# Two-part branch, tile 2's gate/up inside tile 1's second layer, and a last tile in column halves, in a macaron block on one core

## What is computed

```python
def ffn(x):                       # weights ternary, hidden width 512, every linear layer without bias
    h = silu(lin(x, w1) * w1_s) * (lin(x, w2) * w2_s)
    h = gelu(lin(h, h1) * h1_s)   # 512 -> 512
    h = gelu(lin(h, h2) * h2_s)   # 512 -> 512
    return lin(h, w3) * w3_s      # 512 -> 128
x = x + 0.5 * ffn(layernorm(x))
h = layer_norm(layernorm(x), gamma, beta)
k, v = lin(h, Wk) + bk, lin(h, Wv) + bv
w = exp((lin(k, Wka) + bka) / sqrt(128)); w = w / cumsum(w)
x = x + cumsum(w * k) * v         # cumsums along the 256 positions
x = x + 0.5 * ffn(layernorm(x))
```

## Time and profile before

| | us |
|---|---|
| median of 3 runs | 395.91 (395.11 to 396.01) |
| the profiled execution | 396.45 |
| its span in the trace | 394.7 |
| PE busy | 382.2 (97%) |
| DVE busy | 337.2 (85%) |
| ACT busy | 304.7 (77%) |
| POOL busy | 49.9 (13%) |

### The profile page before, as it was taken

How to read it: one execution, slowest core, us unless ns; L and a number is a source line. 1 busy time by engine, 2 the same in 40 slices (tenths; PEclk the granted TensorE clock), 3 DMA queues, 4 the chain that set the end, 5 groups by cost and what they waited for, 6 DMA issues and landing times.

```text
span 394.7 us, 5879 instructions
## 1 busy us (share of the span) xinstructions
PE 382.2 (97%) x1670; PEld 292.7 (74%) x1670; DVE 337.2 (85%) x755; ACT 304.7 (77%) x513; POOL 49.9 (13%) x70
## 2 busy tenths in 40 slices
PE   7789999999999999999999999999999999999995
PEld 2367888777777787777687787777777777778883
DVE  4868778989989899998999899799899989976733
ACT  2767778996896799679779986877898778686763
POOL 4721011110100220101022010100411010020000
PEclk9999999999999999999999999999999999999999
DMA  7700000000000000000000000000000000000001
GB/s 265 261 1 2 0 2 0 1 0 2 0 2 0 0 0 0 0 0 0 0 0 0 0 0 27 0 0 27 0 0 27 0 27 0 27 2 0 27 2 55
DMA packets 3901, 7.45 MB, mean 19 GB/s; under 512 B 560, under 2 KB 1200, under 8 KB 3760
## 3 DMA queue, kind: packets, MB, share of 16 engines
q1 hardware_dynamic: 3168, 6.36, 4.5%
q10 hardware_dynamic: 720, 0.93, 0.7%
HBM read 5.19 MB, written 2.10 MB: 18 GB/s over the span
## 4 chain that ended last, share of the span: by engine, by line
PE 79%; DVE 11%; issue 4%; ACT 4%; POOL 0%; DVEq 0%; ACTq 0%; POOLq 0%
PE hid_ps L385 52%; PE gate_ps L385 6%; PE up_ps L385 5%; PE y_ps L385 5%; DVE rcsum L783 3%; PE y_ps L397 3%; PE xt_ps L397 2%; PE y_ps L521 2%; PE xt_ps L505 2%; DVE gate L700 1%; DVE csum L778 1%; ACT L632 1%; DVE full L710 1%; ACT full L572 1%; PE xt_ps L508 1%
## 5 line engine op out<-in xcount | busy, mean ns | idle before, releaser
L385 PE MATMUL hid_ps<-act_hi,hi_h 128*128 128x512 f32 x512 | 208.9, 408 | 1.0 <-DVE flag_i L661 1.0
L385 PE MATMUL hid_ps<-act_lo,hi_h 128*128 128x512 f32 x512 | 200.1, 391 | 0.0
L719 DVE TENSOR_TENSOR act_lo<-full,act_hi 128x512 fp32r<-128x512 f32 x189 | 124.2, 686 | 27.5 <-ACT act_hi L577 21.9
L572 ACT ACTIVATE full<-hid_ps,vec 128x512 f32<-128x512 f32 x128 | 88.0, 688 | 43.3 <-PE hid_ps L385 38.9
L385 PEld LDWEIGHTS hid_ps<-act_hi,hi_h 128*128 128x128 f32 x512 | 96.2, 188 | 25.3 <-issue 4.9
L385 PEld LDWEIGHTS hid_ps<-act_lo,hi_h 128*128 128x128 f32 x512 | 96.2, 188 | 23.0 <-issue 3.8
L577 ACT ACTIVATE act_hi<-full 128x512 fp32r<-128x512 f32 x128 | 79.4, 629 | 6.6 <-POOL nmr L287 5.3
L285 POOL TENSOR_TENSOR rstd<-veps,half 128x4 f32<-128x4 f32 x24 | 32.0, 1334 | 294.4 <-DVE veps L680 294.4
L710 DVE SCALAR_TENSOR_TENSOR full<-up_ps,s_half,gate 128x512 f32<-128x512 f32 x63 | 47.1, 748 | 1.5
L555 ACT ACTIVATE tanh<-gate_ps,s_half 128x512 f32<-128x512 f32 x63 | 42.4, 683 | 7.5 <-PE gate_ps L385 6.1
L560 ACT ACTIVATE act_hi<-full 128x512 fp32r<-128x512 f32 x64 | 40.2, 627 | 6.7 <-DVE full L710 6.4
(11 more groups left out here) (80 smaller groups left out, 347.9 us busy)
## 6 DMA issues: line engine op xcount, KB each, us to landing
out<-x_sb SPq DMA_DIRECT2D x8, 256.0 KB, 2.0
x_sb<-x SPq DMA_DIRECT2D x1, 1536.0 KB, 6.5
raw_h<-h2t SPq DMA_DIRECT2D x4, 256.0 KB, 6.9
raw_h<-h1t SPq DMA_DIRECT2D x2, 256.0 KB, 5.3
raw_h<-h1t ACTq DMA_DIRECT2D x2, 256.0 KB, 6.7
raw_w<-w2t ACTq DMA_DIRECT2D x1, 256.0 KB, 4.5
raw_w<-w1t SPq DMA_DIRECT2D x1, 256.0 KB, 4.3
x_sb<-x SPq DMA_DIRECT2D x1, 256.0 KB, 6.7
```

Of the source, the lines that this page charges most:

```text
L385: mm = eng.matmul(ps, w, a, start=(first and n == 0), stop=(last and n == len(seq_) - 1))
L572: eng.activation(full23[m % 2][:, :], hid_ps[m % 2][:, :], ACT.Gelu, scale=col("sh1" if n == 2 else "sh2", m)).then_inc(s_gelu[n], 1)
L719: eng.tensor_tensor(act_lo[n][:, m, :], full[m % 2][:, :], act_hi[n][:, m, :].bitcast(F32), ALU.subtract).then_inc(s_lo[n], 1)
```

## The change

It has five parts. **Warm-up**: seven products instead of ten, four at once, two behind the first `veps`, one behind POOL's first power. **Flags**: the weights' bits are looked at by other engines and at other times, with two flags, one for w1, w2, h1 and one for h2, w3; PE branches twice. **Order**: between the two branches stands SECOND_LAYER, in which pass 1's transposes and gate/up products p1.0 to p1.2 lie among pass 0's second layer, whose first two chunks are taken input by input (p2a to p2d, one of the four inputs each). Pass 1's statistics and normalisation move ahead into START on all engines, POOL's norm(1) moves ahead of low1.0, the h2 casts behind the low1's, and pass 1's tile is loaded before h1.2. Pass 1's first-layer result gets buffers of its own ("second"). **Last tile**: chunk 3 of pass 15's third layer, its w3 product, the transposes back, the add and the store are done in two halves of 256 columns; the fourth input of the w3 product is taken in plain float32 straight from the gelu's result (`last_p4_end`), without `high3.3` and `low3.3`; ACT scales one half, DVE the other. **Buffers**: the outputs that the bits stages throw away lie in buffers of later stages.

```diff
-WARM_UP = 10
+WARM_UP = (4, 2, 1)
...
 START = {
     "PE": (
         "",
-        "t p1.0 p1.1 p1.2 p1.3 flag:sum",
+        "t p1.0 p1.1 p1.2 flag:sum1 p1.3",
     ),
     "ACT": (
         "zwait z",
-        "t bits:h1.3 tanh.0 bits:h2.0 tanh.1 high1.0 bits:h2.1 tanh.2 high1.1 bits:h2.3 tanh.3 high1.2 high1.3",
+        "t bits:h1.1 tanh.0 bits:h1.3 tanh.1 bits:h1.2 high1.0 tanh.2 high1.1 zwait z tanh.3 high1.2 1:t high1.3",
     ),
     "DVE": (
         "stats aggr veps bits:w1 norm",
-        "bits:w2 vec:scales t bits:h1.0 bits:h1.1 bits:h1.2 gate.0 up.0 gate.1 up.1 bits:h2.2 gate.2 up.2 bits:w3 "
-        "flag:raise flag:copy gate.3 up.3 low1.3 stats aggr veps",
+        "bits:w2 t vec:scales bits:h1.0 stats gate.0 up.0 aggr veps gate.1 flag:raise1 up.1 flag:copy1 "
+        "gate.2 norm up.2 gate.3 up.3 1:t low1.3",
     ),
 }
+SECOND_LAYER = "p2a.0 p2a.1 t p2b.0 p2b.1 p2c.0 p2c.1 p1.0 p2d.0 p2d.1 p2.2 p1.1 flag:sum2 p2.3 p1.2"
 FIRST_STEP = {
-    "PE": "p2a.0 p2a.1 p2b.0 p2b.1 p2.2 p2.3 t p1.0 p1.1 p3.0 p1.2 p3.1 p1.3 p3.2 p3.3",
-    "ACT": "gelu2.0 high2.0 gelu2.1 high2.1 1:zwait 1:z gelu2.2 high2.2 t gelu2.3 tanh.0 high2.3 tanh.1 high1.0 "
-           "gelu3.0 high1.1 tanh.2 high3.0 gelu3.1 tanh.3 high1.2 high3.1 zwait z gelu3.2 high1.3 high3.2 gelu3.3 "
+    "PE": "p1.3 p3.0 p3.1 p3.2 p3.3",
+    "ACT": "bits:h2.0 bits:h2.1 tanh.0 gelu2.0 high2.0 gelu2.1 high2.1 high1.0 tanh.1 gelu2.2 high2.2 high1.1 gelu2.3 "
+           "tanh.2 high2.3 tanh.3 high1.2 gelu3.0 high3.0 high1.3 gelu3.1 high3.1 zwait z gelu3.2 high3.2 gelu3.3 "
            "high3.3",
-    "DVE": "low2.0 1:norm low2.1 low2.2 t stats low2.3 aggr veps gate.0 up.0 gate.1 up.1 low1.0 low1.1 gate.2 up.2 "
-           "low3.0 gate.3 up.3 low1.2 norm low3.1 low1.3 low3.2 low3.3",
+    "DVE": "bits:h2.2 bits:h2.3 gate.0 up.0 bits:w3 flag:raise2 low2.0 low2.1 flag:copy2 low1.0 gate.1 up.1 "
+           "low2.2 low1.1 gate.2 low2.3 up.2 gate.3 stats up.3 low1.2 aggr veps low3.0 low1.3 low3.1 norm low3.2 low3.3",
 }
 ORDER = {
...
+LAST_STEP = {
+    "PE": "p2.0 p2.1 p2.2 p2.3 p4 p3.0 p3.1 p3.2 dt last:p4a last:p3.0 last:p3.1 last:p4b last:p4c.0 last:p4c.1 "
+          "last:dt.0 last:dt.1",
+    "ACT": "gelu2.0 gelu2.1 high2.0 high2.1 gelu2.2 high2.2 gelu2.3 high2.3 gelu3.0 p4 high3.0 gelu3.1 high3.1 gelu3.2 "
+           "high3.2 last:gelu.0 last:gelu.1 last:delta",
+    "DVE": "low2.0 low2.1 low2.2 low2.3 low3.0 low3.1 dt low3.2 last:delta last:dt.0 last:dt.1",
+}
...
+        act_hi["second"] = sb("act1_hi_second", [P, MC, TOK], F32R)
+        act_lo["second"] = sb("act1_lo_second", [P, MC, TOK], F32R)
...
+        last_hid = [halves(hid_ps[1], 0), halves(gate_ps[0], 1)]
+        last_y = [halves(gate_ps[1], 0), halves(xt_ps, 1)]
+        last_dt = [halves(up_ps[0], 0), halves(up_ps[1], 1)]
...
-            for k in (0, 2):
-                eng.dma_start(part(raw, "h1", k), h1t[:, k * HID:(k + 1) * HID]).then_inc(s_h1[k], 16)
+            eng.dma_start(part(raw, "h1", 0), h1t[:, 0:HID]).then_inc(s_h1[0], 16)
             xload(1, 2, s_x1t)
+            eng.dma_start(part(raw, "h1", 2), h1t[:, 2 * HID:3 * HID]).then_inc(s_h1[2], 16)
...
-            with eng.Fori(0, NT) as t:
+            with eng.Fori(0, NT - 1) as t:
                 eng.wait_ge(s_x1, t + (NT + 1))
                 eng.dma_start(out[:, bass.ds(t * TOK, TOK)],
                               x_sb[:, bass.ds(t * TOK + NT * TOK, TOK)]).then_inc(s_out, 16)
-            eng.wait_ge(s_out, 16 * NT)
+            for h in range(2):
+                eng.wait_ge(s_last_x, h + 1)
+                eng.dma_start(halves(out[:, (NT - 1) * TOK:], h),
+                              halves(x_sb[:, (2 * NT - 1) * TOK:], h)).then_inc(s_out, 16)
+            eng.wait_ge(s_out, 16 * (NT + 1))
...
+            eng.wait_ge(s_z, 1)
             for k in range(MC):
                 hi("h1", k)
             hi("w1", 0)
             hi("w2", 0)
-            hi("h2", 0)
+            norm(1)
             for m in range(POOL_FIRST):
                 low1(m)
-                hi("h2", m + 1)
-            norm(1)
+            for k in range(MC):
+                hi("h2", k)
             hi("w3", 0)
...
+            def last_layer(n, T, k, h):
+                hi, lo = layer(n, T, k, wait=(h == 0))
+                return (halves(hi[0], h), hi[1]), (halves(lo[0], h), lo[1])
+            def last_p3(T, h, general):
+                if h == 0:
+                    eng.wait_ge(s_gelu[3], MC * T + MC - 2)
+                products(last_hid[h], [("h2", k, MC - 1, *last_layer(2, T, k, h)) for k in range(MC)], s_last_p3, general)
+            def last_p4(T, ks, general):
+                for h in range(2):
+                    products(last_y[h], [("w3", k, 0, *last_layer(3, T, k, h)) for k in ks], None, general,
+                             first=(ks[0] == 0), last=False)
+            def last_p4_end(h):
+                eng.wait_ge(s_last_gelu, h + 1)
+                eng.matmul(last_y[h], wblk(raw, "w3", MC - 1, 0), halves(full23[(MC - 1) % 2], h), start=False,
+                           stop=True).then_inc(s_last_p4, 1)
+            def last_back(h):
+                eng.wait_ge(s_last_delta[h], 1)
+                for j in range(SUB // 2):
+                    mm = eng.transpose(last_dt[h][:, j * P:(j + 1) * P], halves(delta, h)[:, j * P:(j + 1) * P], ident[:, :])
+                mm.then_inc(s_last_dt, 1)
+            def flag_sum(layers):
+                eng.wait_ge(s_inexact, layers)
+                if layers == 2:
+                    eng.wait_ge(s_gate, 3)
+                home = hid_ps[0] if layers == 1 else y_ps
+                eng.matmul(home[0:1, 0:1], inexact[:, layers - 1:layers], ones[:, 0:1], start=True,
+                           stop=True).then_inc(s_fps, 1)
...
-            for _ in range(WARM_UP):
-                eng.matmul(y_ps[0:1, 0:seq], ones[:, 0:1], ones[:, :], start=True, stop=True)
-            schedule("PE", stages(False, 0, []), True)
+            def warm_up(n):
+                for _ in range(n):
+                    eng.matmul(y_ps[0:1, 0:seq], ones[:, 0:1], ones[:, :], start=True, stop=True)
+            warm_up(WARM_UP[0])
+            eng.wait_ge(s_ve, 1)
+            warm_up(WARM_UP[1])
+            eng.wait_ge(s_pow, 1)
+            warm_up(WARM_UP[2])
+            schedule("PE", stages(False, 0, []), "start")
             with eng.register("flag") as flag:
                 eng.wait_ge(s_flag, 1)
                 eng.reg_load(flag, flag_i[0:1, 0:1])
                 with eng.If_eq(flag, 0):
-                    schedule("PE", stages(False, 1, [(s_xhi, 1), (s_xlo, 1)]), False)
+                    schedule("PE", stages(False, 1, [(s_xhi, 1), (s_xlo, 1)]), "second")
+                    eng.wait_ge(s_flag, 2)
+                    eng.reg_load(flag, flag_i[0:1, 1:2])
+                    with eng.If_eq(flag, 0):
+                        schedule("PE", stages(False, 2, [(s_xlo, 2)]), "rest")
+                    with eng.Else():
+                        schedule("PE", stages(True, 2, [(s_xlo, 2)]), "rest")
                 with eng.Else():
-                    schedule("PE", stages(True, 1, [(s_xhi, 1), (s_xlo, 1)]), False)
+                    schedule("PE", stages(True, 1, [(s_xhi, 1), (s_xlo, 1)]), "second")
+                    eng.wait_ge(s_flag, 2)
+                    schedule("PE", stages(True, 2, [(s_xlo, 2)]), "rest")
...
+            def last_gelu(T, h):
+                eng.wait_ge(s_last_p3, h + 1)
+                if h == 0:
+                    eng.wait_ge(s_lo[3], MC * T + MC - 2)
+                eng.activation(halves(full23[(MC - 1) % 2], h), last_hid[h], ACT.Gelu,
+                               scale=col("sh2", MC - 1)).then_inc(s_last_gelu, 1)
...
+            def raise_flag(layers):
+                known = ("w1", "w2", "h1") if layers == 1 else ("h2", "w3")
+                for n in known:
+                    eng.wait_ge(s_bits[n], sum(q == n for q, _ in parts))
+                upto = sum(q in ("w1", "w2", "h1") for q, _ in parts) if layers == 1 else len(parts)
+                eng.tensor_reduce(inexact[:, layers - 1:layers], bits[:, 0:upto], AX_X,
+                                  ALU.max).then_inc(s_inexact, 1)
+            def copy_flag(layers):
+                eng.wait_ge(s_fps, layers)
+                home = hid_ps[0] if layers == 1 else y_ps
+                eng.tensor_copy(flag_i[0:1, layers - 1:layers], home[0:1, 0:1]).then_inc(s_flag, 1)
```

More of the change, by code:

```diff
@@ L210, in macaron_block, with first_act @@
             sem(n) for n in ("s_cs", "s_rc", "s_wg", "s_wgk", "s_pool", "s_adelta", "s_at", "s_x2"))
+        def first_act(T):
+            return "second" if isinstance(T, int) and T == 1 else 1
         def act_z(t):
@@ L327, in step @@
                         emit(which, chunk, stage, L)
+                    elif which == "last":
+                        emit("last_" + stage, chunk, 2 * NT - 1, L)
                     elif which.isdigit():
@@ L337, in schedule @@
```

(27 more changed lines are left out.)

63 lines of the change are left out of this document (40 added, 23 removed).

## The result

The changed kernel takes 392.49 us (median of 4 runs, 391.98 to 392.74), the kernel before 395.96 beside it (4 runs, 395.11 to 396.15). The ratio is 0.9916, interval 0.9900 to 0.9931: 3.5 us or 0.9% faster. The forecast was 392.2. The profiled execution took 392.74, where the sum said 392.75. That the two cancel is luck.

The account below looks back on a forecast made before the run. PE was taken to bound the loop, untouched by the change, with gains only at the ends: head 2.6 plus tail 1.1 makes 3.7 us, off the 395.91 median gives 392.2; own range 391.0 to 393.4, 80% range 390.9 to 394.6.

Parts of the forecast that it names:

- the sum: Whole kernel: 2.6 us at the head plus 1.1 at the tail, taking the profiled execution from 396.45 to 392.75 us.
- Head: Kernel start up to step 1: warm-up, first tile and overlapped second layer bring step 1 from 41.26 to 38.7, 2.6 us.
- the wait for up.1: First tile: PE's p1.3 waits for up.1 on DVE and starts at 15.7 instead of 15.97.
- norm to 17.1: Second-layer walk, DVE's queue: gate.2 ends at 16.5, the norm at 17.1, up.2 at 17.85.
- Branches at 0: PE's flag branches: register load hidden under four long records, cost 0; other bound 0.84 us each, 1.7 for two.
- The rival of code that isn't there: Second branch in PE's program: a code fetch exceeding 4.9 us makes the kernel slower; twice 2.7 gives 397.6; chance 0.05.
- The clock stays low: Warm-up: pauses keep PE at 1.2 GHz until p1.0 is over, costing 0.6 to 1.5 us, 393.3; chance 0.10 to 0.12: 0.12.
- Halves bound by weight loads: Last tile: half records take 0.188 us each, 1.9 us worse, 394.1; chance 0.10.
- Tail: Last tile in column halves, 0.12 us a record: last store issued at 390.87 instead of 392.01, gain 1.1 us.
- Loop at 0: Loop between head and tail: expected to carry the head's shift, its other edits costed at nothing.
- The overlap gives nothing: Second layer: POOL's low1 chain and ACT's queue replace PE's old waits; head gives 0.3, total 394.5; chance 0.10.

Follow-up runs that it names:

- e4: Changed kernel with up.2 of the first tile ahead of the second tile's norm in DVE's first queue: 391.16 us.
- e11: Changed kernel with gelu3.2 ahead of ACT's wait for z in the first step: 390.42 us.
- e9: Kernel before the change with only veps moved ahead of up.3 in DVE's loop order: 395.47 us, ratio 0.9994 to the kernel before.
- e6: Changed kernel without any warm-up products: 395.22 us, ratio 0.9970 to the kernel before.
- e1: Changed kernel with its last tile done whole, as before, its store back in SP's loop: 392.44 us, ratio 0.9934 to the kernel before.
- e12: Changed kernel with up.2 ahead of norm, gelu3.2 ahead of z's wait, veps ahead of up.3, second half's store on ACT: 389.46 us.
- e10: Changed kernel with the last tile's store as one transfer from SP's loop, behind both adds: 392.07 us, ratio 0.9911 to the kernel before.

## Why the prediction was right, and where its steps were not

**Head, 2.6 predicted, 2.82 at step 1's start and 2.68 at its transposes: two errors that cancelled.** That the size came out is luck. The start was better than walked. Transposes came at 7.67, not 8.3: x landed 0.12 earlier, z took 0.86 instead of 1.15, and PE was free in time. p1.3 follows p1.0 by 5.44 in every trace with the short warm-up, three pairs and the flag's sum in a row, so the wait for up.1 that I had put into DVE's queue isn't there: the scales took 0.65, not 1.0. p1.3 at 14.38 is 1.3 earlier than predicted. The overlap was worse by 1.1 us: from p1.3 to step 1 it is 24.06 us, where I had 23.0 and before had 25.3. The step that failed is "norm to 17.1": tile 1's z beside POOL's low1 took 1.66. With e4's order the same stretch is 37.76 - 14.64 = 23.1, as walked. The long wait in front of step 1, for a gelu behind `zwait z`, was in the walk, and step 1 came at 38.44 for 38.7; I had seen that wait and not asked who stood behind it, and e11 shows it to be worth more than the norm (1.38 against 0.94). The size also leans on one profile of the kernel before, whose warm-up was 1.0 us longer than e9's: from e9's trace, with its 1.6 us of low clock taken off, the transposes would stand at 45.55 - 1.6 = 43.95, and the head would give 1.75 us, an estimate.

**Branches at 0.** Both traces show no gap at either branch, and one branch less changes nothing. The first branch was not taken out. The rival of code that isn't there has nothing for it.

**The clock stays low.** It didn't: weight loads of the warm-up are 0.43 us apart up to 6.48 and 0.17 to 0.2 from 6.88 on, so the rise came 1.2 us earlier than the 8.1 that the prediction kept.

```profile
6.48 0.13 PEld L602 LDWEIGHTS y_ps<-ones 128*1 128x1 f32 x1 [0.30 <-issue]
6.88 0.30 PEld L602 LDWEIGHTS y_ps<-ones 128*1 128x1 f32 x2 [0.27 <-POOL rstd L318]
```

e6, with no warm-up at all, cost 2.1 to 2.7 us, more than the 0.6 to 1.5 I gave this rival. What I missed is the same mechanism in the kernel before: a low clock behind the gap at the flag, in about half of its executions. Its profile (mean clock 0.999) happens to be one without. Half of 0.9 to 2.2 us, so some 0.5 to 1.1 by estimate, is the share of the gain in the medians, which no row shown could give. That the sum met the profiled execution all the same has other causes: that one took 396.45 with its clock up, with the warm-up 1.0 us longer than in e9's trace and all four rounds 0.4 us long.

**Halves bound by weight loads.** Refuted: 28 records at 0.12 us with a load of 0.19 each that overlaps. The rule of the Trainium skill, page "TensorE: Matmul & The Clock Gate", Part 3, that was weighed in the prediction doesn't hold here. The same part also lets a load be pulled ahead when it targets the background weight buffer, and that, which the prediction left out, would fit the trace.

**Tail, 1.1 predicted.** Up to the last add 1.0, as walked; to the end of the span 0.2 in this pair of traces, 0.4 in the mean of all, and 0.0 to 0.7 in the times of e1. The mis-sized term is the 2.7 us behind the last store's issue, which I had carried over unchanged: it became 3.7 (387.3 to 391.0). Behind the halves the last store meets more of the instruction fetch than behind a whole tail, and the prediction gave that no price.

**Loop at 0.** Right for the change; the trace's 0.84 is POOL's chance.

**The overlap gives nothing.** Refuted: against the kernel before (25.3) the overlap gives 1.2 us between p1.3 and step 1, 2.2 with e4, and 3.5 with e4 and e11 in e12 (27.24 - 5.44 = 21.8 us, against 24.06 in the trace of the change alone).

## What to carry to other kernels

Where a queue written by hand waits for another engine (`zwait z`), look at what stands right behind it: if the bound engine waits for that, one swap of two names can be worth half of what a rebuilt stage is (e11: 1.3 us in the trace, 1.5 to 2.1 in the times). When a chain is shortened to its last instruction, price what follows it too, the store above all: moved earlier, it met another transfer and landed 0.8 us later (e10 against e9). The gap of 2 us on TensorE cost its length here and, in about half of the executions, the clock behind it; closing such a gap may gain more than one profile shows, so read the granted clock of every run beside the profile.
